# When a planned TensorE stream takes its projections and output products: behind values rather than in the middle of score rows

## The chip, the cores and the metric

The kernel runs on one core of a Trainium2 chip. The metric is the device time of one execution in microseconds. Engines: PE is TensorE (its weight loads are shown as PEld), DVE is VectorE, ACT is ScalarE, POOL is GpSimd, SP is SyncE, which issues the DMAs.

## The reference

For x of 2 x 2048 x 256, with 16 query heads, 4 key and value heads and 16 elements a head:

```python
xn = layernorm(x)
q = rope((xn @ wq).reshape(B, S, 16, 16)); k = rope((xn @ wk).reshape(B, S, 4, 16))
v = (xn @ wv).reshape(B, S, 4, 16)
# k, v broadcast to 16 heads; causal mask
attn = softmax(where(causal, einsum('bshd,bthd->bhst', q, k) / sqrt(16), -inf))
att = einsum('bhst,bthd->bshd', attn, v).reshape(B, S, D) @ wo
ffn = real(ifft(fft(xn) @ (w_re + 1j * w_im))) + bias
out = x + att + ffn
```

## The kernel before, in words

The 4096 rows of x are cut into 8 chunks of 512 (four for each batch), and each chunk has four steps, one for each key head with its four query heads: 32 steps. A step of the chunk j of its batch (j from 0 to 3) has 4 (j + 1) units, one for each 128 keys, 320 units in all. For a unit TensorE makes four score matrices, keys by queries (`scores`, line 1340, jobs "b"), ScalarE takes their exponentials into `prob_sb` (line 975), on the diagonal GpSimd masks them (line 859), and TensorE multiplies them with the values (`values`, line 1357, jobs "pv"; eight matmuls in column strips, summed in `psO`). A softmax needs its maximum first, so each step's scores are also made the other way round, queries by keys, one step or more ahead (`a_use`, line 1293, jobs "a", with a mask added by line 1298 on the diagonal); VectorE reduces them to maxima (lines 1102 and 1104), which go by DMA into rows of the q operand (`load_shift`). A pair of jobs "a" fills two banks of `psA` for one reduce.

The scores have a contraction of 48 to 50 rows, so each uses one half of the array's rows, and two of them, one in each half, run side by side. Values use all rows and strips of columns. Projections and output products use the whole array. These are the aside jobs: "t" (transposing the normalised x, line 1258), "qk" (three blocks of q and k for each chunk, line 1266), "v" (line 1273), and for a finished chunk, twice, "e" (transposing the sums back, line 1308), "e2" (line 1317) and two "e3" (`project_out`, lines 1325 and 1327, which multiply by the folded Fourier matrix and by wo). After "t", "qk", "v", "e2" and "e3" ScalarE copies the bank out, in TensorE's order; after "e" VectorE normalises. After "qk" GpSimd turns (six jobs "r", `rotate`), and SyncE stores and loads q and k through HBM. After "e3" GpSimd adds to x (job "add", line 850), for which the bias must have been added (job "bias", line 814), and SyncE stores the output.

Scores and aside jobs share a ring of three `psS` banks, jobs "a" and "e" share two pairs of `psA` banks, and exponentials run at most three units ahead of the values. The order of the jobs on all engines is made before the program is built by `schedule()`, a planner in Python with a cost for each job and clocks of its own for TensorE (`now`), ScalarE (`act`) and VectorE (`dve`). At each turn it picks a job: a score for VectorE while VectorE has less than 1.4 us queued, one for ScalarE while that has less than 1.2 us, values when their exponentials are done, and else an aside job. The list BESIDE limits how many aside jobs are given by the end of each step. GpSimd's jobs have a rank, the smallest goes first: mask 0, add 0.7, r 1.0, n 1.5, ones 2.0, bias 2.5. The first two steps' maxima, and some projections, come before there are any values. In the loop there are 1152 jobs "a", 1152 "b", 320 "pv" and 95 aside jobs.

Of the kernel before, what the change touches and what calls it, by code (L numbers as in the profile page):

```python
# [5 lines left out]
def attention_fourier_block(nc, x, wq, wk, wv, wo, w_re, w_im, bias, dft, rope, out):  # L6
# [79 lines left out]
    def where(g):  # L86
        n = max(m for m in range(STEPS) if BEGIN[m] <= g)
        return n, g - BEGIN[n]
# [21 lines left out]
    def last_late(t, late, turns):  # L110
        return max(at for at in range(late, turns) if (at - late) % (4 + RING) == t)

    def schedule():

        pe, act, dve, pool, dma = [], 0.0, 0.0, [], []
        now, mode, half = 0.0, "", [0.0, 0.0]
# [5 lines left out]
        pool_jobs, dma_jobs = [], []  # L122
# [4 lines left out]
        aside_at, beside, asked = 0.0, 0, 0  # L127
# [12 lines left out]
        def add_pool(ready, rank, job):  # L140
            nonlocal asked
            asked += 1
            pool_jobs.append((ready, rank, asked, job))
# [70 lines left out]
        def run_dma():  # L214
            for job in list(loads):
                cc = job[1] if job[0] == "kload" else job[1] // KV
                gate = stored[3 * cc + 2]
                over = (chunk_begin(NJ) if cc >= KS else 0) if job[0] == "kload" else BEGIN[max(job[1] - 2 * KV + 1, 0)]
                if len(pv_at) < over:
                    continue  # L220
                gate = max(gate, pv_at[over - 1] if over else 0.0)
                if gate <= now:
                    loads.remove(job)
                    issue_dma(gate, job)
            for e in list(waiting_x):
                if e[0] <= now:
                    waiting_x.remove(e)
                    issue_dma(e[0], ("x", e[1]))
            for cc in range(2, CHUNKS):
                if cc not in norms and cc - 1 in xnT_at and cc in x_at and x_at[cc] <= now:  # L230
                    norms.add(cc)
                    add_pool(max(xnT_at[cc - 1], x_at[cc]), 1.5, ("n", cc))

        def full(kind, took, ready):
            nonlocal now, mode
            start = max(now, half[0], half[1], ready) + (0.15 if mode == "half" else 0.0)
            half[0] = half[1] = start + took
            now, mode = start + took - 0.1, kind
            return start + took + 0.12
# [11 lines left out]
        def on_act(end, took, ready=0.0):  # L251
            nonlocal act
            act = max(act, end + 0.07, ready) + took
            return act

        def on_dve(end, took):
            nonlocal dve
            dve = max(dve, end + 0.07) + took
            return dve
# [8 lines left out]
        def take(job, done):  # L268
            bank[job] = len(ring)
            ring.append(done + 0.14)  # L270

        def b_ready():
            g, k = next_b
            if g >= TOTAL:
                return big
            n, u = where(g)
            at = bank_ready()
            if u == 0 and k == 0:
                at = max(at, shifted.get(n, big))
            if k == 0 and g >= DEEP and len(pv_at) <= g - DEEP:  # L280
                at = big
            return at

        def a_ready():
            if next_a >= len(A_USES):
                return big
            return max(slot_ready(), q_ready.get(A_USES[next_a][1], big))

        def v_ready():
            g = next_v  # L290
            if g >= TOTAL or g not in exp_at:
                return big
            n, u = where(g)
            at = exp_at[g]
            if UNITS[n][u][3] is not None:
                at = mask_at.get(g, big)
            if u == 0 and n > 0:
                at = max(at, copied[n - 1] if len(copied) >= n else big)
            if u == len(UNITS[n]) - 1 and n >= OS:
                at = max(at, normed.get(((n - OS) // KV, 1), big))  # L300
            return at
# [24 lines left out]
        def back_ready():  # L326
            if not back:
                return big
            job = back[0]
            cc, h = job[1], job[2]  # L330
            if job[0] == "e":
                return max(copied[KV * (cc + 1) - 1] if len(copied) >= KV * (cc + 1) else big, slot_ready())
            if job[0] == "e2":
                return max(normed.get((cc, h), big), bank_ready())
            return max(on_at.get((cc, h), big), bank_ready())
# [83 lines left out]
        def do_back():  # L419
            job = back[0]  # L420
            ready = back_ready()
            back.pop(0)
            pe.append(job if job[0] != "e" else ("e", len(slots)))
            cc, h = job[1], job[2]
            if job[0] == "e":
                end = full("full", 0.9, ready)
                seq_a.append(job)
                slots.append(on_dve(end, 1.2) + 0.1)
                normed[cc, h] = dve + 0.05
            elif job[0] == "e2":  # L430
                take(job, on_act(full("full", 0.45, ready), 0.53))
                on_at[cc, h] = act + 0.1
            else:
                end = full("full", 1.8, ready)
                take(job, on_act(end, 0.32, adds.get((cc, h - 1, job[3]) if h else (cc - 1, 1, job[3]), 0.0)))
                e3_at[cc, h, job[3]] = end
                add_pool(act + 0.1, 0.7, ("add", cc, h, job[3]))

        add_pool(-4.0, 1.0, ("r", 3, 0))
# [5 lines left out]
        while next_v < TOTAL or back or ahead < CT:  # L445
            if late is None and next_a == len(A_USES) and not stage and not back:
                late = len(ring)
            run_pool(now)
            run_dma()
            ready = {"a": a_ready(), "b": b_ready(), "v": v_ready(), "s": stage_ready(), "e": back_ready()}  # L450
            soon = now + 0.05
            choice = None
            step = min(where(min(next_b[0], TOTAL - 1))[0], STEPS - 1)
            first_s = step in STAGE_FIRST and ready["s"] <= soon
            aside = "s" if first_s else ("e" if ready["e"] <= soon else ("s" if ready["s"] <= soon else None))
            if aside and beside >= BESIDE[step] and min(ready["a"], ready["b"], ready["v"]) < big:
                aside = None
            if next_b[0] >= TOTAL and ahead < CT and (ready["v"] > soon or next_v == TOTAL) and (ring[last_late(ahead, late, len(ring))] <= soon or next_v == TOTAL):
                choice = "x"
            elif a_part == 0:  # L460
                choice = "a" if not (ready["b"] <= soon and pe[-1][0] != "b") else "b"
            elif aside and pe and pe[-1][0] == "pv" and now - aside_at > 2.5 and act - now > 0.5:
                choice = aside
            elif ready["a"] <= soon and dve - now < 1.4:
                choice = "a"
            elif ready["b"] <= soon and act - now < 1.2:
                choice = "b"
            elif ready["v"] <= soon:
                choice = "v"
            elif aside:  # L470
                choice = aside
            elif ready["a"] <= soon:
                choice = "a"
            elif ready["b"] <= soon:
                choice = "b"
            else:
                first = min(ready.values())
                assert first < big, (ready, next_b, next_v, next_a, stage[:1], back[:1])
                choice = min(("a", "b", "v"), key=lambda k: ready[k])
                if ready[choice] > first + 1.0 and (beside < BESIDE[step] or ready[choice] == big):  # L480
                    choice = min(ready, key=lambda k: ready[k])
            if choice in ("s", "e"):
                aside_at = now
                beside += 1
            {"a": do_a, "b": do_b, "v": do_v, "s": do_stage, "e": do_back, "x": do_ahead}[choice]()
        now += 1000.0
        run_pool(now)
        return pe, pool, dma, bank, seq_a, late

    PE_ORDER, POOL_ORDER, DMA_ORDER, BANK, SEQ_A, LATE = schedule()  # L490
    for k, job in enumerate(OPENING):
        BANK[job] = k
# [1007 lines left out]
```

## Time and profile before

| | |
|---|---|
| three runs | 1002.67, 1005.73, 1021.61 us, median 1005.73 |
| the profiled execution | 1008.69 us, span 1006.9 us |
| mean granted TensorE clock | 0.956 |
| TensorE matmul, weight load busy | 961.0 us (95%), 471.1 us (47%) |
| VectorE, ScalarE, GpSimd busy | 737.4 us (73%), 650.7 us (65%), 325.1 us (32%) |
| chain that ended last | TensorE 84%, ScalarE 8%, VectorE 5%, issue 2% |

The span runs from the first to the last instruction. Ends of matmuls are modelled, so a busy TensorE may have waited; starts are measured. A row of a timeline merges neighbouring instructions of one line (x says how many). In it "psS<-q_st,k_st" is a score for ScalarE, "psA<-k_st,q_st" one for VectorE, "psO<-prob_sb,v_sb" values.

### The profile page before, as it was taken

How to read it: one execution, taken by the hardware profiler on the slowest of the kernel's cores; microseconds unless marked ns; L12 is line 12 of the kernel's file. 1: busy time of each engine (PE TensorE's matmuls, PEld its weight loads, DVE VectorE, ACT ScalarE, POOL GpSimd, SP SyncE). 2: the span in 40 equal slices, each digit the busy share in tenths (PEclk: the TensorE clock that was granted, in tenths of full speed). 3: DMA queues.
4: the chain of work that ended last, by engine and by line, in shares of the span. 5: the costliest groups of instructions: out<-in, count | busy, mean ns of one | idle time of the engine just before them, and what ended most of it. 6: DMA issues, size and time to landing. Idle time of an engine off the chain costs nothing.

```text
span 1006.9 us, 17764 instructions
## 1 busy us (share of the span) xinstructions
PE 961.0 (95%) x6792; PEld 471.1 (47%) x6792; DVE 737.4 (73%) x894; ACT 650.7 (65%) x1303; POOL 325.1 (32%) x350
## 2 busy tenths in 40 slices
PE   8989899999999989999999999999999999999998
PEld 6644455445444434443354554544444444544424
DVE  7686677767787787777888776677878887788801
ACT  2433566664676655676777666676767766677785
POOL 6287683868136300133500132327210100100000
PEclk9867699999999996999999999999999997999989
DMA  5645005152211210010200311001510000000000
GB/s 162 138 136 107 23 32 106 44 109 70 67 35 48 58 13 17 12 48 2 68 17 6 64 44 49 12 11 34 95 34 11 2 1 1 12 12 1 1 1 22
DMA packets 37701, 43.50 MB, mean 43 GB/s; under 512 B 11376, under 2 KB 23280, under 8 KB 37616
## 3 DMA queue, kind: packets, MB, share of 16 engines
q1 hardware_dynamic: 37616, 42.36, 17.2%
q8 instruction: 54, 0.88, 0.4%
q14 instruction: 31, 0.25, 0.1%
HBM read 27.13 MB, written 14.68 MB: 42 GB/s over the span
## 4 chain that ended last, share of the span: by engine, by line
PE 84%; ACT 8%; DVE 5%; issue 2%; DMA 0%; SPq 0%; POOL 0%; ACTq 0%
PE psO L1357 28%; PE psA L1293 20%; PE psS L1340 18%; ACT prob_sb L975 6%; PE psS L1266 4%; PE psS L1325 3%; PE psS L1327 2%; DVE pmax L1102 2%; PE psA L1298 2%; DVE pmax L1104 2%; PE psS L1273 1%; PE psA L1308 1%; ACT oraw_sb L984 1%; PE psS L1317 1%; PE psA L1365 1%
## 5 line engine op out<-in xcount | busy, mean ns | idle before, releaser
L975 ACT ACTIVATE prob_sb<-psS 128x512 f32<-128x512 f32 (+2 forms) x1108 | 560.0, 586 | 226.3 <-PE psS L1340 223.6
L1104 DVE TENSOR_REDUCE pmax<-psA 128x2 f32<-128x1024 f32 x384 | 459.9, 1220 | 116.9 <-PE psA L1293 115.7
L1340 PE MATMUL psS<-q_st,k_st 50*128 50x512 f32 (+3 forms) x1232 | 397.9, 432 | 5.2 <-ACT prob_sb L975 4.3
L1293 PE MATMUL psA<-k_st,q_st 48*128 48x512 f32 (+3 forms) x1280 | 360.7, 428 | 15.6 <-DVE pmax L1104 7.0
L1357 PE MATMUL psO<-prob_sb,v_sb 128*17 128x512 f32 (+3 forms) x2560 | 305.8, 551 | 15.5 <-ACT prob_sb L975 7.7
L1293 PEld LDWEIGHTS psA<-k_st,q_st 48*128 48x128 f32 x1280 | 177.9, 193 | 249.1 <-DVE pmax L1104 90.0
L1102 DVE TENSOR_REDUCE pmax<-psA 128x4 f32<-128x512 f32 (+2 forms) x192 | 198.7, 1046 | 87.0 <-PE psA L1298 85.9
L859 POOL TENSOR_SCALAR_AFFINE_SELECT prob_sb<-prob_sb 128x512 f32<-128x512 f32 x128 | 81.1, 635 | 499.2 <-ACT prob_sb L975 487.2
L1340 PEld LDWEIGHTS psS<-q_st,k_st 50*128 50x128 f32 x1232 | 195.0, 192 | 93.7 <-ACT prob_sb L975 83.4
L1357 PEld LDWEIGHTS psO<-prob_sb,v_sb 128*17 128x17 f32 x2560 | 43.2, 96 | 104.4 <-issue 40.9
L1298 PE MATMUL psA<-mask_r,mask_l 64*128 64x64 bf16 (+1 forms) x768 | 80.3, 213 | 0.0
L1266 PE MATMUL psS<-xnT,w_sb 128*128 128x512 f32 x96 | 49.8, 647 | 0.8 <-ACT xnT L930 0.8
L850 POOL TENSOR_TENSOR x_sb<-x_sb,back_sb 128x256 f32<-128x256 f32 x28 | 20.5, 732 | 86.2 <-ACT back_sb L960 82.8
L826 POOL TENSOR_TENSOR turn<-qc,cos_sb 128x512 f32<-128x512 f32 x21 | 26.7, 1272 | 58.1 <-ACT qc L938 56.5
L1298 PEld LDWEIGHTS psA<-mask_r,mask_l 64*128 64x128 bf16 x768 | 39.2, 101 | 12.0 <-issue 3.1
L938 ACT ACTIVATE qc<-psS 128x512 f32<-128x512 f32 x24 | 14.3, 598 | 45.8 <-PE psS L1266 43.8
L960 ACT ACTIVATE back_sb<-psS 128x256 f32<-128x256 f32 x28 | 10.7, 384 | 35.3 <-PE psS L1327 35.3
L1209 DVE RECIPROCAL rl<-psS 128x16 f32<-128x16 f32 x4 | 1.0, 250 | 43.6 <-PE psS L1380 43.6
L1325 PE MATMUL psS<-m_sb,xnT 128*128 128x256 f32 x112 | 31.7, 405 | 0.0
L804 POOL TENSOR_SCALAR xn<-x_sb,stat,rstd 128x256 f32<-128x256 f32 x24 | 29.0, 1218 | 2.6 <-DMA x_sb<-in_L_attn_x 2.5
L1327 PE MATMUL psS<-wo_sb,back_sb 128*128 128x256 f32 x112 | 28.7, 379 | 0.0
L1266 PEld LDWEIGHTS psS<-xnT,w_sb 128*128 128x128 f32 x96 | 17.5, 200 | 23.2 <-issue 18.5
(106 smaller groups left out, 570.3 us busy)
## 6 DMA issues: line engine op xcount, KB each, us to landing
q_st<-parts_scratch SPq DMA_DIRECT2D x174, 64.0 KB, 2.5
parts_scratch<-parts SPq DMA_DIRECT2D x64, 128.0 KB
k_st<-parts_scratch SPq DMA_DIRECT2D x48, 128.0 KB, 4.4
q_st<-spartT SPq DMA_DIRECT2D x256, 2.0 KB
x_sb<-in_L_attn_x SPq DMA_DIRECT2D x7, 512.0 KB, 4.1
out<-x_sb SPq DMA_DIRECT2D x14, 256.0 KB, 2.3
parts_scratch<-parts SPq DMA_DIRECT2D x32, 64.0 KB
oraw_sb<-in_L_attn_x SPq DMA_DIRECT2D x1, 1536.0 KB, 11.7
```

Source lines behind the costliest of these rows:

```text
L804: nc.gpsimd.tensor_scalar(xn[:, i, :], x_sb[:, xt(cc, i), :], stat[:, t, 0:1], rstd[:, t:t + 1], ALU.subtract, ALU.mult).then_inc(S["xn_re ...
L859: nc.gpsimd.affine_select(out=blk, in_=blk, compare_op=ALU.is_ge, fill=0.0, base=0, pattern=[[0, R], [1, P]], channel_multiplier=-1).then_ ...
L975: nc.scalar.activation(prob[:, g % DEEP, r0:r0 + hp, s0:CH], bank_at(bank)[:, 0:hp * w].rearrange("p (h s) -> p h s", h=hp), ACT.Exp).then ...
L1102: nc.vector.reduce_max(to, psA[:, two:two + 2, 0:per * w].rearrange("p o (h s) -> p o h s", h=per), AX.X).then_inc(S["a_free"], 1)
L1104: nc.vector.reduce_max(pmax[:, heads[0]:heads[0] + 3:2, i, q], psA[:, two:two + 2, :], AX.X).then_inc(S["a_free"], 1)
L1266: last = mm(bank, w_sb[:, c, block_cols(m)], xnT[:, cc % XS, c, :], start=(c == 0), stop=(c == KC - 1))
L1293: last = mm(bank[:, k * w:(k + 1) * w], q_st[lo:lo + ROWS, n % (2 * KV), heads[o * per + k] % 2, i * P:(i + 1) * P], k_st[lo:lo + ROWS, sl ...
L1298: last = mm(to, mask_l[lo:lo + HALF, h, :], mask_r[lo:lo + HALF, h:h + 1, :].broadcast_to([HALF, per, HALF]), start=False, stop=h == 1)
L1325: mm(bank[:, 0:D], xnT[:, cc % XS, c, t * P:(t + 1) * P], m_sb[:, c, :], start=(c == 0), stop=False)
L1327: last = mm(bank[:, 0:D], o_nT[:, i, c * P:(c + 1) * P], wo_sb[:, c, :], start=False, stop=(c == KC - 1))
L1340: last = mm(bank[:, h * w:(h + 1) * w], k_st[lo:lo + FULL, key_slot(n, tile), kv, tile % CT * P:(tile % CT + 1) * P], q_st[lo:lo + FULL, n ...
L1357: last = mm(psO[GW * r:GW * r + VW, s0:CH], v_sb[:, key_slot(n, tile) * CT + tile % CT, n % KV, :], prob[:, g % DEEP, r, s0:CH], start=(u ...
```

## The change

Three edits in the planner; no instruction is added or taken away, only orders change.

- When all of scores for VectorE, scores for ScalarE and values are held back or not ready, an aside job is given only if TensorE's last job was not a score, so behind values or another aside job. Before, it was given behind anything. The last branch stays: if nothing is ready at once, and the next score or values is more than 1 us later than what else is ready, the planner may still give the aside job there.
- Straight behind values, an aside job is given if more than 2.5 us have passed since the start of the last one. Before, ScalarE had to have more than 0.5 us queued as well.
- When an output product ("e3") is planned, the bias addition of its chunk, if still waiting, gets rank 0.6, ahead of the add (0.7) and of r, n and ones.

```diff
@@ do_back @@
                 e3_at[cc, h, job[3]] = end
+                for k, e in enumerate(pool_jobs):
+                    if e[3] == ("bias", cc):
+                        pool_jobs[k] = (e[0], 0.6) + e[2:]
                 add_pool(act + 0.1, 0.7, ("add", cc, h, job[3]))
...
             elif a_part == 0:
                 choice = "a" if not (ready["b"] <= soon and pe[-1][0] != "b") else "b"
-            elif aside and pe and pe[-1][0] == "pv" and now - aside_at > 2.5 and act - now > 0.5:
+            elif aside and pe and pe[-1][0] == "pv" and now - aside_at > 2.5:
                 choice = aside
             elif ready["a"] <= soon and dve - now < 1.4:
                 choice = "a"
...
             elif ready["v"] <= soon:
                 choice = "v"
-            elif aside:
+            elif aside and pe[-1][0] not in ("a", "b"):
                 choice = aside
```

## Rows read from the trace of the kernel before

**Rows 1.** The page's granted TensorE clock, forty slices, in tenths.

```profile
PEclk9867699999999996999999999999999997999989
```

**Rows 2.** The page's groups of ScalarE exponentials and VectorE maxima; mean ns of one.

```profile
L975 ACT ACTIVATE prob_sb<-psS 128x512 f32<-128x512 f32 (+2 forms) x1108 | 560.0, 586 | 226.3 <-PE psS L1340 223.6
L1104 DVE TENSOR_REDUCE pmax<-psA 128x2 f32<-128x1024 f32 x384 | 459.9, 1220 | 116.9 <-PE psA L1293 115.7
```

**Rows 3.** The waits of TensorE's weight loads: us in total, times, longest.

```profile
PEld psS L1340 <- ACT prob_sb L975: 83.4, 209, 1.7
...
PEld psO L1357 <- ACT prob_sb L975: 35.7, 107, 1.8
...
PEld psO L1357 <- POOL prob_sb L859: 7.8, 25, 0.4
```

**Rows 4.** TensorE's timeline from 869 us: start, length, line, out<-in, count.

```profile
870.13 0.50 PE L1340 MATMUL psS<-q_st,k_st 50*128 50x512 f32 x2
870.56 0.65 PE L1317 MATMUL psS<-ident,back_sb 128*128 128x128 f32 x4
...
874.84 0.41 PE L1357 MATMUL psO<-prob_sb,v_sb 128*17 128x128 f32 x8
875.18 1.13 PE L1325 MATMUL psS<-m_sb,xnT 128*128 128x256 f32 x4
...
877.11 0.33 PE L1293 MATMUL psA<-k_st,q_st 48*128 48x128 f32 x1
...
878.38 1.05 PE L1357 MATMUL psO<-prob_sb,v_sb 128*17 128x512 f32 x8
879.36 0.50 PE L1293 MATMUL psA<-k_st,q_st 48*128 48x512 f32 x2
...
880.03 1.13 PE L1325 MATMUL psS<-m_sb,xnT 128*128 128x256 f32 x4
...
881.96 0.50 PE L1293 MATMUL psA<-k_st,q_st 48*128 48x512 f32 x2
...
882.62 0.62 PE L1357 MATMUL psO<-prob_sb,v_sb 128*17 128x512 f32 x4
```

**Rows 5.** The same timeline: values groups from 130 us and at 992 us.

```profile
130.54 0.63 PE L1357 MATMUL psO<-prob_sb,v_sb 128*17 128x256 f32 x8
...
131.76 0.41 PE L1357 MATMUL psO<-prob_sb,v_sb 128*17 128x128 f32 x8
...
134.46 1.05 PE L1357 MATMUL psO<-prob_sb,v_sb 128*17 128x512 f32 x8 [0.45 <-ACT oraw_sb L984]
...
137.82 1.05 PE L1357 MATMUL psO<-prob_sb,v_sb 128*17 128x512 f32 x8
...
992.08 1.05 PE L1357 MATMUL psO<-prob_sb,v_sb 128*17 128x512 f32 x8
```

**Rows 6.** Six steps: window, length, busy us of PE, PEld, DVE, ACT, POOL; clock, DMA.

```profile
432.40:480.90 48.50, 47.50 (x316) 20.01 (x312) 37.75 (x37) 33.61 (x67) 20.50 (x19) 1.00 0.10 30
480.90:521.50 40.60, 39.88 (x321) 18.27 (x318) 34.71 (x39) 30.70 (x62) 13.33 (x14) 1.00 0.13 39
521.50:561.40 39.90, 39.13 (x352) 19.27 (x349) 33.60 (x43) 30.53 (x61) 2.54 (x4) 1.00 0.05 13
698.30:732.20 33.90, 33.58 (x248) 16.22 (x247) 26.81 (x29) 23.70 (x48) 11.49 (x13) 1.00 0.46 96
732.20:766.00 33.80, 32.59 (x245) 15.70 (x242) 25.71 (x28) 23.82 (x49) 4.74 (x7) 1.00 0.08 24
766.00:795.30 29.30, 29.05 (x212) 12.37 (x213) 25.69 (x26) 22.38 (x46) 2.54 (x4) 1.00 0.01 2
```

**Rows 7.** ScalarE's timeline from 874 us, idle time before in brackets.

```profile
874.25 1.58 ACT L975 ACTIVATE prob_sb<-psS 128x512 f32<-128x512 f32 x3
877.22 0.39 ACT L960 ACTIVATE back_sb<-psS 128x256 f32<-128x256 f32 x1 [1.38 <-PE psS L1327]
```

**Rows 8.** GpSimd's bias additions, groups by line; mean ns of one.

```profile
L814 POOL TENSOR_TENSOR x_sb<-x_sb,bias_sb 128x1024 f32<-128x1024 f32 x8 | 19.0, 2374 | 0.1
```

## The prediction

> **What bounds the kernel now.** I read the granted clock first. It is nine tenths or more in each of the page's forty slices but the second to fifth, the 16th, the 34th and the 39th [rows 1]. The windows by step come next [rows 6]: TensorE is busy 96 to 99% of every step that I cut out, VectorE 76 to 88%, ScalarE 69 to 77%. So TensorE sets the pace, but that busy time hides waits, since the ends of matmuls are modelled: a matmul of 512 columns is drawn some 0.5 us long, while the next of its half can start 0.23 us later. The view that tells the truth is TensorE's timeline, read by the distance from one start to the next [rows 4, 5]. There I cut the stream into intervals, each from the start of one values group (line 1357) to that of the next, and take off the values and the aside job. What is left is the time of the rows of half-array scores. The waits view names what the rows wait for: in its weight loads, whose idle time shows a wait early, a score waits for ScalarE to free a bank in 209 cases, the values for the exponentials in 107 [rows 3]. One exponential of 512 columns is 0.59 us and one reduce of two banks 1.22 us [rows 2], so a full unit (four exponentials, and about two reduces) needs 2.3 us of ScalarE and 2.4 us of VectorE, and TensorE's own work on it, 0.98 us of values and a row of eight scores (four to each half), is hardly less. Where no aside job stands in an interval the three are about even and TensorE waits a little for the other two.
>
> **What an aside job costs by itself.** It takes the same time behind values as behind scores: an output product is 1.93 us from 875.18 to the row at 877.11, behind values, and 1.93 us from 880.03 to 881.96, behind scores [rows 4]. So the move changes only what lies around it.
>
> **What one break of a row costs.** A row of two scores (one to each half) takes 0.43 us, from 870.13 to 870.56. One of four takes 0.66 us, from 881.96 to 882.62 [rows 4]. A further pair is thus 0.23 us, and what is left, 0.20 us, is paid once for each row, however long. Putting the aside behind the values joins two rows and takes one such 0.20 us away; the way from values to the aside costs no more than that from values to scores, 0.34 us after a values group of 128 columns at 874.84 [rows 4]. The Trainium skill, "TensorEngine Tiling (Array Packing)", section Key Properties, says that changing the tiling mode drains TensorE. The 0.20 us agrees with that, and by the rule alone the change is a plain gain: one change of mode less for each aside moved, which is the first rival below.
>
> **How many are moved.** Of the 95 aside jobs of the loop, 58 stand behind a score, 36 behind values and one behind another aside. Seven of the 58 stand in the first four steps or ahead of them, where there are few values to stand behind, or none. The planner's last branch still gives such a job when everything else is more than 1 us off. So about 50 move, and 50 x 0.20 = 10 us is the most that the saved breaks can bring. That is the gain's end of the range for this term.
>
> **What the break buys now.** An aside in the middle of a row is given when both VectorE (1.4 us or more) and ScalarE (1.2 us or more) have work queued and the values aren't ready, so it stands where TensorE would wait. The timeline shows this. From step 4 on there are 41 intervals with one aside in mid-row, the first from 134.46 to 137.82, the last from 878.38 to 882.62 [rows 4, 5]. Their row time, both parts and the break together, is 1.44 us for 7.8 scores, 185 ns a score, with hardly any wait in it: the last has 0.67 us (879.36 to 880.03) and 0.66 us for four scores each. There are 29 with the aside behind values, the first from 131.76 to 134.46, the last from 874.84 to 878.38. They take 1.65 us for 7.0 scores, 236 ns a score, though their row isn't broken. The last of them has 1.27 us for seven scores (877.11 to 878.38), where 0.20 us and 3.5 pairs of 0.23 us would give 1.0 us. And 227 intervals without any aside, the first from 130.54 to 131.76, the last ending at 992.08, take 1.56 us for 7.0 scores, 223 ns a score [rows 5]. So a row behind an aside behind values waits as much as a plain one, and the broken one doesn't wait. The reason is in ScalarE's timeline: its three exponentials last from 874.25 to 875.83, then it is idle for 1.38 us under the values and the product, and the values at 878.38 need an exponential that TensorE could feed only after 877.11 [rows 7]. Three banks of scores are 1.8 us of ScalarE's work; values and an output product together are up to 2.9 us.
>
> **The sum.** The bounds for one moved aside are -0.20 us (break saved, no wait comes back) and (236 - 185) x 7.8 = +0.40 us (its rows come to look like those behind values). Between them I go by whole steps, where all work is counted whatever its place. Of the steps of 16 units, the two without asides last 40.6 and 39.9 us; the one from 432.4 lasts 48.5 us with six asides, five of them behind scores, whose own time is 2 x 0.59 (transposes) + 3 x 1.91 (projections) + 1.93 = 8.8 us; 48.5 - 8.8 = 39.7 us, 0.6 us less than the mean of the two. Of those of 12 units, the one without asides lasts 29.3 us, and the two with four asides each (seven of the eight behind scores, own time 1.02 + 0.59 + 2 x 1.93 = 5.5 us) last 33.9 - 5.5 = 28.4 and 33.8 - 5.5 = 28.3 us [rows 6]. So 12 broken rows go with 0.6 + 0.9 + 1.0 = 2.5 us less than no asides would, 0.2 us for each. That is as coarse as the steps themselves, of which two alike differ by 0.7 us, and a step is cut wherever its first score falls, so I take two thirds of it, 0.13 us. An aside behind values I take at its own time, since its row waits like a plain one. Moving 50 then costs 50 x 0.13 = +6.5 us.
>
> **The other edits.** Dropping the condition that ScalarE has over 0.5 us queued gives asides behind values also where ScalarE is about to run dry. It is what makes the move possible; its cost is within the +0.40 end, as the last behind-values interval above shows such a case. The bias addition on GpSimd (2.37 us, eight of them [rows 8]) is put ahead of the rotations once an output product of its chunk is planned. Behind it may be queued a mask, which the values wait for; such waits are 7.8 us in all now [rows 3]. At worst one mask a chunk comes 2.4 us later, at best nothing changes, for the bias must be added anyway: I take 0, with 0 to +2 us. Stores, loads and the shift DMAs keep their order on SyncE but for when outputs are ready; the deadlines of the projections are a step or more away: 0, within 1 us either way.
>
> The profiled execution took 1008.7 us, so the sum is 1008.7 + 6.5 = 1015.2 us on its scale. That execution was 3.0 us above the median of 1005.7, so against the median I say **1012 us**. The measurement can tell about 2% (20 us) from no change.
>
> **The rivals.**
> 1. Row breaks saved, nothing lost. For it: the 0.20 us is seen at every change, 50 times; scores that were held back for the aside are issued before the values, so ScalarE and VectorE have fuller queues under values and aside. Against it: the 29 existing cases. Half to all of the 10 us: 996 to 1001, 999 us.
> 2. Slower by a starved ScalarE. Place: the first row behind values and a long aside. Price: +0.40 us each, 50 x 0.40 = +20 us, 1026 us. It decides wherever ScalarE's queue at the end of the values is shorter than the aside (1.9 us for projections and products, 55 of the 95). For it: the 1.38 us idle [rows 7] and that the condition against just this goes. Against it: VectorE and ScalarE catch up later, having a quarter of their time free in steps with asides.
> 3. The change does little: with ScalarE or VectorE full and the values not ready, the planner's last branch still gives the aside in mid-row, so only half move. 1006 to 1009 us.
> 4. A further or a missing stretch at half clock. The 16th slice (from 378 us) and the 34th (from 831 us) lie at the two joins where the long chunks of both batches begin [rows 1]; if the order moves a wait there, such a stretch comes or goes. It widens the others and has no time of its own.
>
> **Chances and range.** Forecast (1005 to 1018 us) 0.45; rival 1 0.30; rival 2 0.15; rival 3 0.10. Over 2% slower (above 1026) only the upper half of rival 2: 0.08. Over 2% faster (below 985) needs more than every break and half of today's waits, 0.02. The rest, 0.90, is within 2%. The range goes from 996, which takes in nearly all of rival 1, to 1024, which leaves out the upper half of rival 2.
>
> **What would show it.** In the changed profile: asides follow values in some 85 of 95 cases; the number of score rows falls by about 50; a moved aside has the same own time; the row behind it is longer than 0.20 + 0.23 us a pair by about 0.3 us, with the values waiting for the exponentials. In the waits view, the idle time of the weight loads of the values grows (35.7 us now), while that of steps without asides stays. If instead that idle time stays and rows only get fewer, rival 1 holds. The prediction is wrong if the steps without asides change, or if the opening (before step 2) changes by more than 5 us.

## The result and the profile after

The changed kernel takes 1050.9 us (median of 4, 1044.5 to 1051.2) against 1007.9 us for the one before: ratio 1.045, 95% interval 1.036 to 1.054. It is 43 us slower, and the forecast was 1012 us with a range to 1024. Its profiled execution took 1044.5 us (span 1042.7 us, mean granted clock 0.949). The ratios leave out runs that lie more than 1.5% above the fastest of their kernel.

The page of the changed kernel, granted clock, and its groups of exponentials and maxima (they answer to [rows 1] and [rows 2]):

```profile
PEclk9878699998999997999999999999999998999999
...
L978 ACT ACTIVATE prob_sb<-psS 128x512 f32<-128x512 f32 (+2 forms) x1108 | 555.7, 591 | 195.5 <-PE psS L1343 191.4
L1107 DVE TENSOR_REDUCE pmax<-psA 128x2 f32<-128x1024 f32 x384 | 456.4, 1219 | 149.6 <-PE psA L1296 149.0
```

The single operations cost what they did. The half-clock time worked out from the mean clocks is 2 x (1 - 0.949) x 1042.7 = 106 us, before 2 x (1 - 0.956) x 1006.9 = 89 us. The profiled execution is the fastest of the changed kernel. The others have mean clocks of 0.931 to 0.938, which is 130 us or more at half clock, and take 1050.9 us or more. So 6 of the 43 us lie outside what the profile shows and go with further half-clock time.

The waits of TensorE's weight loads after (beside [rows 3]):

```profile
PEld psS L1343 <- ACT prob_sb L978: 102.3, 260, 2.2
...
PEld psO L1360 <- ACT prob_sb L978: 39.3, 113, 1.8
...
PEld psO L1360 <- POOL prob_sb L862: 8.7, 25, 1.9
```

The scores' waits for a bank that ScalarE must free have grown from 83.4 to 102.3 us, the values' waits hardly (35.7 to 39.3 us).

The same place in the stream as the last intervals of [rows 4], TensorE's timeline, and ScalarE's beside [rows 7]:

```profile
896.31 1.05 PE L1360 MATMUL psO<-prob_sb,v_sb 128*17 128x512 f32 x8
897.29 1.13 PE L1328 MATMUL psS<-m_sb,xnT 128*128 128x256 f32 x4
...
899.22 0.50 PE L1296 MATMUL psA<-k_st,q_st 48*128 48x512 f32 x1
...
900.89 1.05 PE L1360 MATMUL psO<-prob_sb,v_sb 128*17 128x512 f32 x8
901.88 1.13 PE L1328 MATMUL psS<-m_sb,xnT 128*128 128x256 f32 x4
```

```profile
895.17 2.06 ACT L978 ACTIVATE prob_sb<-psS 128x512 f32<-128x512 f32 x4
899.32 0.39 ACT L963 ACTIVATE back_sb<-psS 128x256 f32<-128x256 f32 x1 [2.09 <-PE psS L1330]
899.76 2.07 ACT L978 ACTIVATE prob_sb<-psS 128x512 f32<-128x512 f32 x4
903.91 0.39 ACT L963 ACTIVATE back_sb<-psS 128x256 f32<-128x256 f32 x1 [2.09 <-PE psS L1330]
```

Values and an output product follow each other for 2.91 us (896.31 to 899.22) and no score is made. ScalarE has used up its banks at 897.2 (895.17 + 2.06) and is idle for 2.09 us, and so again behind the next values. The row that follows takes 1.67 us for eight scores and four small mask matmuls. VectorE's timeline in step 12, at another such place, shows the same:

```profile
419.01 0.95 DVE L1105 TENSOR_REDUCE pmax<-psA 128x2 f32<-128x768 f32 x1
422.46 2.36 DVE L1107 TENSOR_REDUCE pmax<-psA 128x2 f32<-128x1024 f32 x2 [2.50 <-PE psA L1296]
426.98 2.35 DVE L1107 TENSOR_REDUCE pmax<-psA 128x2 f32<-128x1024 f32 x2 [2.17 <-PE psA L1296]
```

In the intervals shown each engine is idle for 2 us or more, and then has the work of a whole row to do at once.

**Where the 37 us of the loop are.** I cut the streams of both kernels into rows, values and asides, as in the prediction, and took for a row 0.19 us, 0.24 us a pair of full scores and 0.045 us for each small mask matmul, for the rest its own time. What a piece lasts beyond that is wait; a piece that is mostly at half clock counts to the half-clock stretches. Before: 375 rows, 772.6 us of own time, 120.9 us of wait at full clock, and 57.5 us more in half-clock stretches, 951.0 us in all. After: 323 rows, 759.3, 164.8 and 63.6 us, 987.7 us. So own time fell by 13 us and waits at full clock rose by 44. Of the 13 us, 52 x 0.19 = 10 us are the price of a row that the account itself puts in, so they are no new measurement of it. Of the 44 us, 24 came in rows behind an aside and 19 in rows behind values, which the prediction had left as they were. The border between the two kinds of wait isn't sharp: if every piece that touches a half-clock stretch is counted there, waits at full clock rise by about 20 us and the stretches by about 26.

The intervals of the prediction, cut from the changed kernel from step 4 on, say the same without a model. Some 80 have one aside behind values and take 221 ns a score; some 220 have none and take 235, where they took 223 before. So the moved asides lost the 185 ns a score of their old place, 36 ns x 7.8 = 0.28 us each or 14 us for 50, and the plain rows became longer by 12 ns for 7.2 scores in 222 intervals, 19 us.

**In which steps they are.** Step 4 begins at 129.8 us before and at 135.2 us after, step 12 at 381.4 and 403.4 us. So of the 36 us between the two spans 5 lie ahead of step 4, 17 in steps 4 to 11 and 14 from step 12 on. The windows of steps 4 to 11, before and after:

```profile
129.80:381.40 251.60, 241.30 (x1738) 116.38 (x1736) 193.66 (x206) 161.60 (x325) 123.80 (x117) 0.99 0.25 58
```

```profile
135.20:403.40 268.20, 252.88 (x1723) 121.12 (x1724) 194.01 (x205) 159.29 (x323) 120.79 (x114) 0.95 0.23 54
```

The work is nearly the same, and the clock is lower (0.95 beside 0.99). The longest new wait stands ahead of step 8, whose scores for ScalarE can't begin before its maxima have landed in q (`load_shift`, eight DMAs). In the changed kernel no aside is given there, the next one only behind the values at 253.18 us. TensorE makes scores for VectorE alone from 243.8 to 249.6 us, at VectorE's pace, ScalarE is idle for 7.70 us, and half clock begins at 247.9 us:

```profile
242.44 5.28 SPq L713 DMA_DIRECT2D q_st<-spartT  x8
...
250.34 0.60 ACT L978 ACTIVATE prob_sb<-psS 128x512 f32<-128x512 f32 x1 [7.70 <-PE psS L1343]
```

Before, four asides stood over the same eight DMAs, none of them behind values, and the step's first score came at 238.21 us:

```profile
229.81 5.31 SPq L710 DMA_DIRECT2D q_st<-spartT  x8
...
230.68 1.09 PE L1308 MATMUL psA<-ident,oraw_sb 128*128 128x128 f32 x8 [0.74 <-ACT oraw_sb L984]
231.61 1.90 PE L1273 MATMUL psS<-w_sb,xnT 128*128 128x64 f32 x16
...
234.27 0.66 PE L1317 MATMUL psS<-ident,back_sb 128*128 128x128 f32 x4
...
236.29 1.13 PE L1325 MATMUL psS<-m_sb,xnT 128*128 128x256 f32 x4
```

By the account the changed kernel's row, from 243.8 to 253.2 us, has 6.2 us of wait, the row of before that begins at 238.21 us 1.0 us. This is lost cover too, but of a wait for maxima and their DMAs.

Windows by step after, beside [rows 6] (step 13, 14, then chunk 6, steps 24 to 27), and the two of before that are not shown there, steps 12 and 27:

```profile
458.10:507.30 49.20, 47.79 (x306) 19.75 (x302) 35.10 (x35) 33.28 (x66) 30.41 (x27) 0.97 0.11 33
507.30:548.40 41.10, 40.23 (x314) 19.00 (x310) 34.44 (x38) 30.32 (x61) 2.54 (x4) 0.96 0.06 20
...
728.20:769.10 40.90, 39.73 (x266) 20.63 (x267) 26.79 (x33) 24.87 (x52) 5.46 (x8) 1.00 0.06 18
769.10:798.60 29.50, 28.51 (x217) 12.44 (x217) 25.16 (x26) 22.40 (x46) 2.54 (x4) 1.00 0.03 11
798.60:827.60 29.00, 28.06 (x208) 11.95 (x209) 24.17 (x26) 22.30 (x46) 2.54 (x4) 1.00 0.01 2
827.60:865.70 38.10, 34.20 (x240) 14.85 (x241) 33.39 (x34) 23.20 (x47) 2.54 (x4) 0.95 0.01 2
```

```profile
381.40:432.40 51.00, 50.59 (x321) 23.90 (x317) 36.70 (x40) 32.86 (x65) 4.73 (x7) 0.88 0.04 12
...
795.30:828.20 32.90, 30.74 (x224) 13.16 (x226) 28.35 (x30) 23.21 (x47) 2.54 (x4) 1.00 0.01 2
```

Steps without asides are as they were (29.0 us beside 29.3), but one. Step 24 has eight asides behind values, and VectorE is busy 66% of it (26.8 of 40.9 us) where it was 79% of the old one (26.8 of 33.9). In step 27, before the long chunk begins, the planner gives VectorE 58 jobs against 50, VectorE is busy 88%, and the step takes 38.1 us instead of 32.9. That this is work put off in step 24 isn't shown. In the first run below step 24 has eight asides as well and takes 40.6 us, but step 27 has 43 jobs and takes 30.8 us; and with both engines' work halved step 27 still is 4 us longer than in the old order. It is the planner's order of the scores that makes step 27 longer.

### The profile page after: what moved, and what is told of

Its sections match the earlier page's. It is cut to its first block, busy times and chain, and to the rows that moved or that the text cites. A ratio compares the mean times of both kernels' runs of the same rounds, so it can differ in the third digit from the quotient of the medians.

```text
span 1042.7 us, 17762 instructions
## 1 busy us (share of the span) xinstructions
PE 984.8 (94%) x6792; PEld 484.3 (46%) x6792; DVE 730.6 (70%) x894; ACT 647.2 (62%) x1303; POOL 324.6 (31%) x350
## 4 chain that ended last, share of the span: by engine, by line
PE 79%; ACT 10%; DVE 6%; issue 3%; SPq 1%; DMA 1%; POOL 0%; ACTq 0%; POOLq 0%; DVEq 0%
PE psO L1360 26%; PE psS L1343 16%; PE psA L1296 16%; ACT prob_sb L978 8%; PE psS L1269 5%; DVE pmax L1107 3%; PE psS L1328 3%; DVE pmax L1105 2%; PE psS L1330 2%; PE psA L1301 2%; PE psA L1311 2%; PE psS L1276 1%; ACT oraw_sb L987 1%; PE psA L1403 1%; PE psS L1261 1%
## 5 line engine op out<-in xcount | busy, mean ns | idle before, releaser
L1343 PE MATMUL psS<-q_st,k_st 50*128 50x512 f32 (+3 forms) x1232 | 417.7, 434 | 11.7 <-ACT prob_sb L978 10.2
L1296 PE MATMUL psA<-k_st,q_st 48*128 48x512 f32 (+3 forms) x1280 | 356.7, 425 | 23.2 <-DVE pmax L1107 12.5
L1343 PEld LDWEIGHTS psS<-q_st,k_st 50*128 50x128 f32 x1232 | 201.9, 191 | 120.0 <-ACT prob_sb L978 102.3
L1360 PEld LDWEIGHTS psO<-prob_sb,v_sb 128*17 128x17 f32 x2560 | 43.3, 96 | 102.6 <-ACT prob_sb L978 39.3
L1212 DVE RECIPROCAL rl<-psS 128x16 f32<-128x16 f32 x4 | 1.0, 250 | 41.9 <-PE psS L1383 41.9
L1328 PEld LDWEIGHTS psS<-m_sb,xnT 128*128 128x128 f32 x112 | 19.0, 189 | 22.9 <-ACT prob_sb L978 20.4
```

What stands on the lines that cost most here:

```text
L1296: last = mm(bank[:, k * w:(k + 1) * w], q_st[lo:lo + ROWS, n % (2 * KV), heads[o * per + k] % 2, i * P:(i + 1) * P], k_st[lo:lo + ROWS, sl ...
L1328: mm(bank[:, 0:D], xnT[:, cc % XS, c, t * P:(t + 1) * P], m_sb[:, c, :], start=(c == 0), stop=False)
L1343: last = mm(bank[:, h * w:(h + 1) * w], k_st[lo:lo + FULL, key_slot(n, tile), kv, tile % CT * P:(tile % CT + 1) * P], q_st[lo:lo + FULL, n ...
L1360: last = mm(psO[GW * r:GW * r + VW, s0:CH], v_sb[:, key_slot(n, tile) * CT + tile % CT, n % KV, :], prob[:, g % DEEP, r, s0:CH], start=(u ...
```

## The experiments

Each time is a median, and the kernel before was run beside it on the same chip.

**One edit at a time.** The bias edit by itself changes no order at all. Without it the dropped condition would put an addition of chunk 0 ahead of its bias, so it stays in the first run.

```diff
-            elif aside and pe and pe[-1][0] == "pv" and now - aside_at > 2.5 and act - now > 0.5:
+            elif aside and pe and pe[-1][0] == "pv" and now - aside_at > 2.5:
```

> Only the condition on ScalarE's queue is dropped (with the bias edit, which alone changes no order); the branch for mid-row asides is as before. Of the 95 asides 20 stand behind scores, 75 behind values (before: 58 and 36). Theory 1 (lost cover: an aside behind values costs its waits wherever it is): 38 asides moved at 43/50 = 0.86 us each, +33 us, 1041. Theory 2 (ScalarE run dry, because the condition is gone): nearly the whole loss, +35 to +43 us, 1043 to 1050. Theory 3 (the ban on mid-row asides does the harm, since TensorE now stands still where it filled waits): under +15 us. Theory 4 (chance of the order: half-clock stretches): anywhere, but the step windows without a half-clock stretch would be as before.

Measured 1030.3 us, ratio 1.020 (1.014 to 1.027), +20 us. Theories 1 and 2 were too high, theory 3 (under 15) too low. The condition alone is nearly half of the loss.

```diff
-            elif aside:
+            elif aside and pe[-1][0] not in ("a", "b"):
```

> Only the ban on asides behind scores; the condition that ScalarE has over 0.5 us queued is kept for the early branch. Behind scores stand 25, behind values 56, behind another aside 14. Theory 1 (lost cover): 33 moved, but 13 of them behind another aside, +20 to +28 us, 1028 to 1036. Theory 2 (ScalarE run dry): +0 to +10 us, since ScalarE has work queued when an aside is given. Theory 3 (the ban does the harm): +35 us or more.

Measured 1170.9 us, ratio 1.159 (1.149 to 1.168), +160 us, which no theory had so large. The window of the 100 us from 620 us:

```profile
620.00:720.00 100.00, 73.31 (x342) 36.82 (x341) 74.02 (x86) 9.56 (x20) 6.26 (x9) 0.57 0.17 35
```

ScalarE is busy 10 us of 100, and the clock is 0.57. The order of step 19 holds 129 scores for VectorE in one row, for steps 22 to 25 and so up to two chunks ahead. The planner is caught in its own rules there: the values of the last unit of step 18 are planned only once the sums of the last finished chunk are normalised, for which a job "e" must be given. The ban holds that job back behind every score, and without values no exponentials are planned more than three units ahead. The row ends only when all such scores are made. Step 19 takes 99.7 us for 9.1, and step 27 93.7 us for 32.9. With the condition dropped as well (the whole change) asides come soon enough behind values, and that harm is gone.

**The opposite.** The old rules, but the early branch is shut (ScalarE would need 50 us queued):

> The opposite of the change: the branch that gives an aside straight behind values is shut, so 92 asides stand behind scores and 3 behind values. Theory 1 (an aside in mid-row covers waits worth more than the break of 0.20 us): 34 more in mid-row at -0.2 to -0.86 us each, -7 to -29 us, 979 to 1001. Theory of the broken rows (each break is a loss and the change's loss came otherwise): +7 us, 1015.

Measured 1098.4 us, ratio 1.086 (1.078 to 1.094). Both theories fell. The loss is again in steps 19 (84.0 us) and 27 (51.5 us), where 134 and 76 scores for VectorE stand, and the job "e" that step 18 needs is again given too late, here without any ban. The run can't tell what more mid-row places are worth: steps 24 to 26 have their scores for VectorE made already in step 19, and over the loop the waits at full clock are 121.7 us beside 120.9.

**Place alone.** The order of before is replayed, each aside that stood behind a score held back to the next values:

```diff
+            if choice in ("s", "e"):
+                if (order and order[-1] in ("a", "b") and kind in MOVE and "v" in order) or held:
+                    held.append(choice)
...
+            if choice == "v" and held:
+                order.append(held.pop(0))
```

> The order of all scores and values is the old one, job for job; only each aside that stood behind a score once values had begun is taken out and put behind the next values. Behind scores stand 3, behind values 84, behind another aside 8. Theory 1 (lost cover, by place alone): 55 moved at 0.5 to 0.86 us, +27 to +47 us, 1035 to 1055. Theory 5 (the loss comes from how the planner reshuffles scores and values around the new places, not from the places): under +12 us.

Measured 1168.8 us, ratio 1.158 (1.150 to 1.166), which is no measure of the place. TensorE waits up to 16.7 us at once for masks, since the replay had planned GpSimd's jobs anew and put whole rotations ahead of masks. The mended run keeps GpSimd's and SyncE's old order and moves only from step 12 on:

> Place alone, mended: the old order of scores, values, GpSimd's and SyncE's jobs, and only the aside jobs that stood behind a score are put behind the next values, from step 12 on (32 of them; steps before 12 as before). Theory SV: each costs 0.4 to 0.9 us more, +13 to +29 us, all of it in steps 12 to 29. Theory 5 (the planner's reshuffling of scores and values makes the loss): within 6 us of before.

Measured 1034.9 us, ratio 1.020 (1.013 to 1.028): +20 us for 32 moved asides, 0.6 us each. The profiled execution is the slowest of the four. In it steps 4 to 8, 10 and 11, ahead of the first moved aside, are as before within 0.2 us; steps 1 and 9, also ahead of it, had further half-clock stretches and were 3.5 and 3.8 us longer. This is the place alone, and it costs, but not what the place cost in the whole change: from step 12 on the span grows by 24 us here and by 14 us there. In steps 4 to 11, where the whole change lost 17 us, the place alone wasn't tried. The rows' account of its profiled execution, whose span is 31 us longer than that of before: 32 rows fewer, -6 us of own time, +30 us of wait at full clock, +8 in half-clock stretches.

**Which engine runs dry.** Half of the exponentials' columns, or half of the columns under each maximum, are left out, in both orders:

```diff
-    nc.scalar.activation(prob[:, g % DEEP, r0:r0 + hp, s0:CH], <bank>, ACT.Exp)
+    nc.scalar.activation(prob[:, g % DEEP, r0:r0 + hp, s0:s0 + w // 2], <bank>[:, :, 0:w // 2], ACT.Exp)
...
-    nc.vector.reduce_max(pmax[:, heads[0]:heads[0] + 3:2, i, q], psA[:, two:two + 2, :], AX.X)
+    nc.vector.reduce_max(pmax[:, heads[0]:heads[0] + 3:2, i, q], psA[:, two:two + 2, 0:CH // 2], AX.X)
```

> The old order; each exponential covers only the first half of each head's columns (the other half of the probabilities is left out; two small memsets at the start), so ScalarE takes about 0.33 us for one instead of 0.59. To be read beside the next run. If ScalarE's queue sets the waits of the old order at all, this is 30 to 90 us faster than the kernel before.

> The changed order with the same half exponentials. Theory S (ScalarE runs dry under values and a long aside, and the values behind the next row wait for its exponentials): the loss of 43 us shrinks to under 12 us against the half-exponential kernel of the old order. Theory V (VectorE runs dry and its maxima fall behind): the loss stays at 30 us or more. Theory C (half-clock stretches, 18 us more of them): stays near 10 to 20 us.

> The old order; each maximum is taken over the first half of the keys of its tile only (so the shift is that of half the keys), and VectorE takes about 0.7 us instead of 1.22. To be read beside the next run. Faster than before by 20 to 60 us if VectorE's pace sets waits in the plain rows.

> The changed order with the same half maxima. Theory S: the loss against the half-maximum kernel of the old order stays at 30 us or more. Theory V: it shrinks to under 12 us. If both engines have a part, it lies between, 12 to 30 us, here and with half exponentials alike.

Measured with half exponentials: old order 972.1 us, changed 1004.7, difference 32.7 us. With half maxima: 1003.0 and 1044.8, difference 41.9 us. The last median is no firm number: the four runs are 1031.4, 1042.2, 1047.4 and 1051.8 us, and the two within 1.5% of the fastest give 1036.8, a difference of 34 us. The old order gained 39 us with half exponentials, inside the 30 to 90 expected, and 8 us with half maxima, where 20 to 60 were expected. Theory S falls by the half exponentials (32.7 us, not under 12), theory V by the half maxima (34 us or more, not under 12), and that each engine has a part of its own (12 to 30 us in both) falls too: halving either leaves most of the loss. Theory C had 10 to 20 us and falls by its number. But half-clock time is not out of it: by the mean clocks the runs with half exponentials have 82 us of it in the old order and 121 in the changed one, in the median. Both were then halved together:

> The old order with half exponentials and half maxima together (the other halves are left out). Halving one engine's work left most of the loss, 32.7 us with half exponentials and 41.9 us with half maxima. To be read beside the next run.

> The changed order with both halved. Theory SV (under values and a long aside ScalarE and VectorE both run dry, and the row behind waits for whichever of them is left slow): the loss against the old order with both halved falls to 10 us or less, and may turn into a gain of up to 10 us, the breaks saved. Theory O (the loss lies in TensorE's order itself, for example pairs of scores that fall into the same half, or in transfers): it stays at 25 us or more.

Measured 948.7 us (ratio to before 0.936, 0.931 to 0.942) and 957.4 us (0.945, 0.939 to 0.952): the difference falls from 43 to 8.7 us. The half-clock time is the same in both orders, 72 and 73 us in the median, so the further half-clock stretches went as well. The groups of the changed order with both halved show what the engines then cost:

```profile
L978 ACT ACTIVATE prob_sb<-psS 128x256 f32<-128x256 f32 (+2 forms) x1108 | 353.1, 373 | 293.2 <-PE psS L1345 283.9 <-PE psA L1345 0.5
...
L1107 DVE TENSOR_REDUCE pmax<-psA 128x2 f32<-128x512 f32 x384 | 257.3, 688 | 273.6 <-PE psA L1298 271.1 <-PE psA L1303 0.9
```

So 0.59 us became 0.37 and 1.22 became 0.69, and most of the loss went with them. That one alone took off so little fits a row that waits for whichever of the two is still slow. Cut at steps 4 and 12, the profiled executions show where the loss went (us by which the span is longer than in the old order with the same work; with both halved, step 4 begins at 123.1 and 130.2 us, step 12 at 362.4 and 376.3):

| | ahead of step 4 | steps 4 to 11 | from step 12 on |
|---|---|---|---|
| whole change | +5.4 | +16.5 | +13.9 |
| whole change, both halved | +7.1 | +6.8 | -0.8 |
| place alone, from step 12 | +3.8 | +3.9 | +23.7 |

The third row shows how far such a number can move without any change, ahead of its first moved aside: 4 us. From step 12 on nothing is left of the loss. Ahead of step 4 it stays, and no run looks for its cause. In steps 4 to 11 the wait ahead of step 8 stays: its first score waits for the same eight DMAs, at 238.3 us.

> The kernel that moves only 32 aside jobs behind values from step 12 on (old order otherwise), now with half exponentials and half maxima as in the two both-half runs. Theory SV: the 20 us that the move cost at full work fall to 4 us or less against the old order with both halved (948.7 us), and the 32 breaks saved may turn it to -6 us. Theory R (time is lost because later jobs are delayed, whatever the two engines do): 12 us or more stay.

Measured 959.1 us, ratio 0.945 (0.939 to 0.951), so 9 to 10 us more than the old order with both halved (on another chip, and by the ratios 9), where place alone had cost 20 at full work. It lies between the two theories: about half went. Of the rest a part may be GpSimd's. TensorE's waits for masks, first in the old order with both halved, then in this run:

```profile
PE psO L1359 <- POOL prob_sb L859: 5.0, 8, 1.8
```

```profile
PE psO L1391 <- POOL prob_sb L891: 10.6, 15, 2.0
```

GpSimd's queue is unchanged, so a rotation whose projection was held back can stand ahead of a mask, and the mask, with values behind it, waits too: 5.6 us more. But this profiled execution took 970.7 us, 12 us above the median, with 20 us at half clock in steps 16 and 17 that the old order doesn't have. How much of the 9 us the masks make in a usual run, and what makes the rest, isn't settled.

**The other way, for a faster kernel.**

```diff
-            elif ... and now - aside_at > 2.5 and act - now > 0.5:
+            elif ... and now - aside_at > 2.5 and act - now > (0.5 if {"s": stage[:1], "e": back[:1]}[aside][0][0] in ("t", "e", "e2") else 1.2):
```

> The old rules, but straight behind values a projection or output product is given only if ScalarE has over 1.2 us queued (short ones over 0.5 as before): 77 asides behind scores, 15 behind values, 3 behind another. Theory SV: long asides leave the places where they run both engines dry, 15 to 20 of them at -0.3 to -0.6 us, -5 to -12 us, 996 to 1004. If the old mix is already the best of both, within 5 us.

Measured 1006.3 us beside 1015.3: ratio 0.991 (0.987 to 0.995), 9 us faster than before, clear of noise but under the 2% that counts as a change here, and the fastest kernel that computes everything. The gain is that of theory SV (-5 to -12 us). Two projections or products stand straight behind values where 22 stood, and its 19 rows more cost less than the waits they cover. Steps 20 to 23 alone are 11 us shorter (86.3 beside 97.1 us).

> Old rules, but outside steps 0 to 3 and 16 to 19 an aside straight behind values needs over 1.2 us queued on ScalarE: 85 asides behind scores, 8 behind values, 2 behind another. If mid-row is the cheaper place for short asides too, 3 to 8 us below the run with only long asides so treated; if short ones cost nothing behind values, the same as that or up to 5 us slower, for the breaks.

Measured 1011.5 us, ratio 1.000 (0.997 to 1.003), outside both expectations: the gain is gone. Two things differ from the run above, the short asides outside steps 0 to 3 and 16 to 19 and the long ones inside them, and the mean clocks (0.936 to 0.948 beside 0.952 to 0.958) show more half-clock time, so the run doesn't price the place of a short aside.

> Old rules, but an aside straight behind values is given only if VectorE too has over 0.5 us queued (ScalarE over 0.5 as before): 59 behind scores, 33 behind values, 3 behind another. Theory SV: nearly the old order, so within 6 us of the kernel before.

Measured 1013.2 us, ratio 1.001 (0.998 to 1.005), the same as before, as expected of nearly the same mix.

## Why the prediction was wrong

- **How many move, and what else moves:** right. 87 asides stand behind values (85 foreseen), rows went from 375 to 323, an output product behind values still takes 1.93 us (897.29 to 899.22), and step 2 begins at 103.4 us, before at 103.0.
- **The break:** nothing speaks against the 0.20 us. Rows of two and of four scores still take 0.43 and 0.66 us in the changed kernel, and there are 52 rows fewer. But no run measures the saving by itself, since the 13 us of the account are for the most part this price put in.
- **"An aside behind values I take at its own time, since its row waits like a plain one"** is the step that failed. Step 13 by the prediction's own sum: 49.2 us less five asides of 2 x 0.59 + 3 x 1.91 = 6.9 us is 42.3 us, against 40.3 for steps without asides, so +0.4 us for each of the five above its own time, where I had 0. (3 us at half clock are in it.) The row behind it does wait like a plain one, 221 ns a score beside 235. But the plain rows themselves became longer, from 223 to 235 ns a score, 19 us, a term that the sum didn't have. I read it so: a plain row waits because ScalarE and VectorE are behind, and gives them work meanwhile; behind a dry stretch they have just lost 2 us, and the debt is handed on to later rows. That from step 12 on the loss is gone with both engines halved bears this out. Which row pays for which stretch isn't shown.
- **The sum's one term, 50 x 0.13 = +6.5 us,** was too small even for the row itself: the intervals give 0.28 us for each moved aside, 14 us. Together with the 19 us of the plain rows that is 33 of the 36 us between the profiled executions.
- **The rest of the order.** I priced only the 50 places. The planner also shifted scores and asides between steps: step 27 got 8 more scores for VectorE and 5 us, and the wait for the maxima ahead of step 8 lost the four asides that filled it.
- **Rival 2** had the right place but named ScalarE alone and asked 0.40 us for each move, +20 us. Measured were +43 us for the whole and 0.6 us for each moved aside by place alone (e11). The 1.38 us idle of [rows 7] was its evidence, and I set it aside with "VectorE and ScalarE catch up later". They don't: where no aside stands, each has 2.3 to 2.4 us of work for an interval of about 2.5 us.
- **The whole-step estimate** (0.13 us of cover) rested on 12 broken rows and differences of 0.6 to 1.0 us, as coarse as the steps. The upper bound from the intervals, +0.40 us, was nearer the truth.
- **Rival 1** is refuted: if its 10 us are there, they lie beneath 44 us of waits. **Rival 3** is refuted by the 87 places. **Rival 4** has a part: between the profiled executions half-clock time rose by 17 us, of which the account puts 6 us into the loss, and the median run of the changed kernel has 25 us more of it and is 6 us longer. In steps 4 to 11, with the long waits there, it rose from 5 to 29 us.
- **The signs to look for:** I said the values' waits would grow. It was the scores' waits for a bank. I said that a change in a step without asides would prove the prediction wrong, and step 27 did.
- **Drains.** The rule of the Trainium skill, "TensorEngine Tiling (Array Packing)", section Key Properties, that a change of tiling mode drains TensorE, agrees with the 0.20 us that a row costs beside its scores; no run tells a drain from another fixed cost of a row. As a rule for where to put the asides it points the wrong way here.

What stays open: why the place alone keeps 9 us with both engines halved; what makes the 5 to 7 us ahead of step 4, which halving doesn't touch; and how the loss of the whole change splits between places and reshuffled scores, since the steps before 12, with 22 of the 36 us, weren't tried with places alone.

## What to carry to other kernels

When an engine with a small backlog of buffers behind it (here three banks, 1.8 us) is kept from feeding others, the length of the stretch without new work counts, not the number of mode changes in it. Values (1.0 us) and a product (1.9 us) back to back ran both followers dry, and as these had hardly any slack in the intervals between, the loss wasn't caught up. Look also at the joins between steps, where the next scores wait for something that takes a fixed time (here eight DMAs): work that can be done there is worth keeping for it. When one follower is named as the bound, halve each alone and both together before believing it. And a price read from a few cases of a place isn't the price when every case stands there.

## What the runs showed that I had not expected

Small changes of a planner's rule have cliffs. Two of them (the ban alone, and the shut early branch) let TensorE run two chunks ahead with one kind of score and cost 160 and 88 us. The ban alone left it at half clock for most of a 100 us window (0.57), though its longest idle time between 612 and 689 us, as the profile draws it, was 2.3 us, and all of it there 23.6 us. With half exponentials the old order gains 39 us, with half maxima 8 us, with both 67 us.
